# A transformer decoder layer on one core: all preparation two batches ahead and spread over four units, the first maxima cut on VectorE among zeros, the end worked by blocks, sums together behind the GELUs

## What is computed

```python
x = x + attn(_layernorm(x), wq, wk, wv, wo)          # rope, causal softmax
x = x + xattn(_layernorm(x), ctx_1024, ctx_1024, Wq, Wk, Wv, Wo, bq, bk, bv, bo)
x = x + ffn(_layernorm(x), W1, b1, W2, b2, scale)
# xattn, per batch and head (HEAD_DIM = 8, 256 queries, 1601 keys):
scores = jnp.einsum('bhqd,bhkd->bhqk', Q, K) * scale
attn = jax.nn.softmax(scores, axis=-1)
ctx = jnp.einsum('bhqk,bhkd->bhqd', attn, V)
# ffn: m1, m2 are outer products of tokens 1..16 of the batch
h = einsum(x, W1) + scale * einsum(x, m1) + b1
h = gelu(h)
out = einsum(h, W2) + scale * einsum(h, m2) + b2
```

## Time and profile before

| | |
|---|---|
| times of three runs | 397.19, 403.4, 404.17 us; median 403.4 |
| the profiled execution | 398.09 us, of it a span of 396.2 us from the first to the last instruction |
| TensorE's mean granted clock in it | 0.974 |
| busy share of the span | PE 91%, DVE 77%, ACT 75%, POOL 33% |
| clock at half | 55.98 to 69.6 us, and 342.7 to 349.5 us |

### The profile page before, as it was taken

One profiled execution on the slowest core, in us unless ns is written; L12 is line 12 of the kernel. 1 busy time (PEld: TensorE's weight loads), 2 busy tenths in 40 slices (PEclk: granted clock), 3 DMA queues, 4 the chain that ended last, 5 costly groups with the idle time before them and its releaser, 6 DMA issues.

```text
span 396.2 us, 11681 instructions
## 1 busy us (share of the span) xinstructions
PE 359.5 (91%) x4652; PEld 164.6 (42%) x4652; DVE 304.6 (77%) x694; ACT 298.3 (75%) x637; POOL 131.7 (33%) x204
## 2 busy tenths in 40 slices
PE   7777869989999989999998999999989999899976
PEld 3343433444543444444444434443434434253334
DVE  3566977779899988799998788999977999671022
ACT  1433246878889799889898798797998998859923
POOL 7711940389120206899200124373000037000010
PEclk9999985999999999999999999999999999789999
DMA  8366398013562212236400331114003310000000
GB/s 298 105 170 187 141 248 309 17 58 120 172 178 69 80 31 68 57 127 216 145 2 2 108 98 31 32 48 163 30 2 99 109 58 2 0 16 2 2 2 15
DMA packets 22300, 35.79 MB, mean 90 GB/s; under 512 B 1700, under 2 KB 19790, under 8 KB 22246
## 3 DMA queue, kind: packets, MB, share of 16 engines
q1 hardware_dynamic: 22246, 35.05, 28.4%
HBM read 19.25 MB, written 11.96 MB: 79 GB/s over the span
## 4 chain that ended last, share of the span: by engine, by line
PE 57%; DVE 16%; ACT 13%; issue 5%; POOL 4%; DMA 3%; SPq 0%; ACTq 0%; DVEq 0%; POOLq 0%
PE wsum L1053 20%; PE score L1067 13%; DVE part_max L722 11%; PE ring L1026 9%; PE ring L1087 9%; ACT probs L909 6%; DMA k_unit<-k_rows 2%; ACT q_unit L920 2%; POOL k_parts L570 2%; ACT prob_self L940 1%; PE ring L1112 1%; DMA x_all<-x 1%; PE ring L1137 1%; ACT hidden L997 1%; PE ring L1098 1%
## 5 line engine op out<-in xcount | busy, mean ns | idle before, releaser
L722 DVE TENSOR_REDUCE part_max<-ring 128x1 f32<-128x401 f32 x512 | 259.6, 567 | 35.9 <-PE ring L1087 34.4
L909 ACT ACTIVATE probs<-score 128x512 f32<-128x512 f32 (+1 forms) x416 | 222.6, 597 | 38.7 <-PE score L1067 34.9
L1087 PE MATMUL ring<-k_unit,q_unit 51*128 51x401 bf16 x512 | 141.6, 345 | 5.3 <-ACT v_aug L965 1.2
L1053 PE MATMUL wsum<-probs,v_unit 128*32 128x256 f32 (+1 forms) x1664 | 135.4, 394 | 2.1 <-ACT unit_ctx L914 2.1
L1067 PE MATMUL score<-q_unit,k_unit 51*128 51x256 bf16 (+1 forms) x832 | 124.0, 279 | 7.5 <-ACT probs L909 5.2
L1067 PEld LDWEIGHTS score<-q_unit,k_unit 51*128 51x128 bf16 (+1 forms) x832 | 47.4, 97 | 100.7 <-ACT probs L909 62.6
L1087 PEld LDWEIGHTS ring<-k_unit,q_unit 51*128 51x128 bf16 x512 | 47.7, 95 | 24.8 <-DVE part_max L722 13.2
L1053 PEld LDWEIGHTS wsum<-probs,v_unit 128*32 128x32 f32 (+1 forms) x1664 | 38.7, 109 | 41.5 <-issue 24.5
L570 POOL TENSOR_TENSOR max_parts<-neg_max,c_sb 128x8 bf16<-128x8 f32 x16 | 3.3, 209 | 130.9 <-DVE neg_max L726 130.8
L650 POOL TENSOR_SCALAR prob_norm<-prob_self,prob_rsum 128x128 f32<-128x128 f32 (+1 forms) x12 | 9.0, 763 | 42.9 <-DVE prob_rsum L802 42.9
L920 ACT ACTIVATE q_unit<-ring 3x512 bf16<-3x512 bf16 x32 | 18.5, 579 | 3.4 <-PE ring L1098 3.2
(11 more groups left out here) (115 smaller groups left out, 292.0 us busy)
## 6 DMA issues: line engine op xcount, KB each, us to landing
k_unit<-k_rows SPq DMA_DIRECT2D x32, 300.2 KB
v_unit<-v_aug SPq DMA_DIRECT2D x16, 234.0 KB, 6.7
ctx_sb<-ctx_t SPq DMA_DIRECT2D x4, 800.5 KB, 10.7
k_rows<-k_parts SPq DMA_DIRECT2D x3, 601.5 KB, 3.2
k_rows<-k_parts SPq DMA_DIRECT2D x3, 599.2 KB, 4.1
even<-ffn_rows SPq DMA_DIRECT2D x3, 512.0 KB, 3.9
q_unit<-q_rows SPq DMA_DIRECT2D x30, 48.0 KB
k_rows<-k_parts SPq DMA_DIRECT2D x3, 401.0 KB, 4.2
```

What stands on the lines that cost most here:

```text
L722: v_.tensor_reduce(part_max[:, par, q, head, hp, c:c + 1], ring[s][:, 0:CW], AX.X, ALU.max)\
L909: a_.activation(probs[0:rows, i % PB, :], score[i % EB][0:rows, :], ACT.Exp)\
L1053: last = mm(wsum[32 * j:32 * j + 32, 0:S], v_unit[0:rows, u, VQ * t + VW * j:VQ * t + VW * j + 32], probs[0:rows, i % PB, S * (j // 2):S * ...
L1087: mm(ring[s][:, 0:CW], q_unit[rows, u, hp, P * q:P * (q + 1)], k_unit[rows, u, L * hp + (CW - 1) * c:L * hp + (CW - 1) * c + CW], start=Tr ...
```

## The change

The preparation of batches 2 and 3, which stood one batch ahead for self-attention and two batches ahead for keys, values and rotary parts, now stands wholly two batches ahead, spread over the four quarters: offset 2 everywhere. Batch 1's self-attention goes into the start, among the 32 M of unit 0; its `x2T`, `q`, `split` and `store1` into unit 0 (`SIDE_FIRST`). So the units of batches 2 and 3 have no preparation left. New waits keep the single buffers safe. The load of the next batch's first keys and queries is an item of its own, `fetch`. The row maximum of self-attention is an item of its own, `rowmax`. `AHEAD` and `COUNT` are laid out anew. The first `neg_max` is cut into parts on VectorE instead of GpSimd, and 8 and 4 dummy multiplications of zeros stand ahead of and behind the first mT, instead of 2 ahead. Where the GELU's items stand, the three sums PV that would follow one by one stand together behind them (`sums_due`). At the end, `low0` is halved into two items, each hidden block `g0` to `g3` has a buffer and a GELU of its own, and the last product takes the blocks one by one, with two stores.

```diff
 SIDE = {
...
-    (1, 0): [("prep", "K2", 2)], (1, 1): [("prep", "wo", 1), ("post", "x3T", -1)], (1, 3): [("prep", "K3", 2)],
...
+    (1, 0): [("prep", "store0", 2)], (1, 1): [("prep", "e0", 2), ("prep", "e1", 2), ("prep", "rowmax", 2)],
+    (1, 2): [("post", "x3T", -1)], (1, 3): [("prep", "K2", 2)], (1, 4): [("prep", "soft", 2)],
+    (1, 6): [("prep", "pn", 2)], (1, 7): [("prep", "K3", 2)], (1, 8): [("prep", "v", 2)], (1, 9): [("prep", "fetch", 1)],
+    (1, 10): [("prep", "pT0", 2), ("prep", "pT1", 2)], (1, 11): [("post", "low", -1)],
...
+    (3, 0): [("ctx", 3), ("prep", "V3", 2)], (3, 3): [("post", "h0", -1), ("post", "h1", -1)], (3, 8): [("post", "out", -1)],
 }
+
+SIDE_FIRST = {0: [("prep", "x2T", 1)], 1: [("prep", "q", 1)], 4: [("prep", "split", 1)], 8: [("prep", "store1", 1)]}
...
-FIRST = [("keep", 20), ("ln1", 0), ("ln1", 1), ("xT", 0), ("qk", 0), ("qks", 0), ("K0", 0), ("K1", 0), ("keep", 5),
-         ("e0", 0), ("e1", 0), ("soft", 0), ("pn", 0), ("K2", 0), ("K3", 0), ("store0", 0), ("v", 0), ("xT", 1), ("keep", 6),
-         ("qk", 1), ("pT0", 0), ("pT1", 0), ("av", 0), ("store1", 0), ("wo", 0), ("U0", 0), ("U1", 0), ("U2", 0), ("U3", 0),
-         ("keep", 3), ("ln2", 0), ("x2T", 0), ("q", 0), ("split", 0), ("qks", 1), ("keep", 3), ("pick", 0),
-         ("U4", 0), ("U5", 0), ("U6", 0), ("load", 0), ("keep", 2)]
-BETWEEN = (("K0",), ("K1",), ("K2",), ("K3", "store0"), ("V0",), ("V1",), ("V2",), ("V3", "store1"))
-POST_LAST = ["OT", "Wo", "keep", "ln3", "x3T", "low0", "low1", "h0", "h1", "keep", "out"]
-KEEP_LAST = (10, 3)
-AHEAD = (14, 13, 7, 10)
-AHEAD_FIRST = 6
...
+FIRST = [("keep", 20), ("ln1", 0), ("ln1", 1), ("xT", 0), ("qk", 0), ("qks", 0), ("K0", 0), ("K1", 0), ("v", 0), ("xT", 1),
+         ("e0", 0), ("e1", 0), ("rowmax", 0), ("soft", 0), ("qk", 1), ("qks", 1), ("pn", 0), ("K2", 0), ("K3", 0),
+         ("store0", 0), ("keep", 4), ("pT0", 0), ("pT1", 0), ("av", 0), ("store1", 0), ("wo", 0),
+         ("e0", 1), ("e1", 1), ("U0", 0), ("U1", 0), ("ln2", 0), ("rowmax", 1), ("x2T", 0), ("q", 0), ("split", 0),
+         ("U2", 0), ("U3", 0), ("pick", 0), ("U4", 0), ("U5", 0), ("U6", 0), ("load", 0), ("soft", 1), ("v", 1)]
+BETWEEN = (("K0",), ("V0",), ("V1",), ("pn",), ("K1",), ("V2",), ("pT0",), ("pT1",), ("K2",), ("av",), ("V3",), ("wo",),
+           ("K3", "store0"), (), (), ())
+POST_LAST = ["OT", "Wo", "keep", "ln3", "x3T", "low0", "low1", "low2", "g0", "g1", "g2", "g3", "last"]
+KEEP_LAST = 10
+AHEAD = (14, 13, 11, 12)
+AHEAD_FIRST = 8
...
...
+def sums_due(v, t):
+    here, g = gelu_at(v), KT * v + t
+    since = [g - KT * w - gelu_at(w) for w in (v - 1, v) if 0 <= w and gelu_at(w) is not None and KT * w + gelu_at(w) <= g]
+    if here == t:
+        due = range(g - 3, g)
+    elif any(d in (1, 2) for d in since):
+        due = ()
+    else:
+        due = range(g - 3, g - 2)
+    return [("PV", *divmod(i, KT)) for i in due if i >= 0]
...
-    for i in range(MU // 4):
-        plan += [("M", 0, k) for k in range(4 * i, 4 * i + 4)] + [("prep", name, 1) for name in BETWEEN[i]]
+    for i in range(MU // 2):
+        plan += [("M", 0, 2 * i), ("M", 0, 2 * i + 1)] + [("prep", name, 1) for name in BETWEEN[i]]
     plan += [("ctx", 2)]
-    return plan + [("M", 1, k) for k in range(4)] + [("keep", 2), ("mT", 0)] + [("M", 1, k) for k in range(4, AHEAD_FIRST)]
+    return plan + [("M", 1, k) for k in range(4)] + [("keep", 8), ("mT", 0)] + [("M", 1, k) for k in range(4, AHEAD_FIRST)] + [("keep", 4)]
...
-                        if b:
-                            load_keys(b, 0)
-                            load_queries(b, 0)
-                        else:
+                        if b == 0:
                             load_rest(b)
+                    elif name == "fetch":
+                        load_keys(b, 0)
+                        load_queries(b, 0)
                     elif name == "load":
                         load_values(b, 0)
...
+                    if v == 0:
+                        dve.wait_ge(unit_max_done, 1)
+                        v_.tensor_copy(max_parts[:, :, 0], neg_max[:, 0, :]).then_inc(max_split, 1)
+                        dve.wait_ge(max_split, 1)
+                        v_.tensor_tensor(max_rest[:, :], neg_max[:, 0, :], max_parts[:, :, 0], ALU.subtract)\
+                            .then_inc(max_split, 1)
+                        dve.wait_ge(max_split, 2)
+                        v_.tensor_copy(max_parts[:, :, 1], max_rest[:, :]).then_inc(max_split, 1)
+                        dve.wait_ge(max_split, 3)
+                        v_.tensor_tensor(max_parts[:, :, 2], max_rest[:, :], max_parts[:, :, 1], ALU.subtract)\
+                            .then_inc(max_split, 1)
...
-                if kind == "M" and item[2] == MU - 1:
+                if kind == "M" and item[2] == MU - 1 and item[1]:
                     v = item[1]
                     pool.wait_ge(unit_max_done, v + 1)
-                    if v:
-                        s, n = RING["mT", v - 1]
-                        pool.wait_ge(drained[s], n + 1)
+                    s, n = RING["mT", v - 1]
+                    pool.wait_ge(drained[s], n + 1)
...
+                elif name[0] == "g":
+                    j = int(name[1])
+                    s, n = take(item)
+                    a_.activation(hidden[:, j, :], ring[s][:, 0:S], ACT.Gelu, bias=W("b1")[:, j:j + 1])\
+                        .then_inc(drained[s], 1)
...
+                elif name == "last":
+                    for j in range(FJ):
+                        for needed in ("low2", "g0") if j == 0 else (f"g{j}",):
+                            slot, m = RING["post", needed, pb]
+                            pe.wait_ge(drained[slot], m + 1)
+                        for q in range(QT):
+                            last = strips(score[1 + q][:, 0:D], hidden[:, j, P * q:P * (q + 1)],
+                                          w2_all[:, D * j:D * (j + 1)], start=j == 0, stop=j == FJ - 1)
+                            if j == FJ - 1:
+                                last.then_inc(last_sums, 1)
 
             pe.wait_ge(still_set, 1)
             keep(PLAN[0][1])
```

119 lines of the change are left out of this document (73 added, 46 removed).

## The result

The change is slower: 415.6 us (median of 4 runs, 413.0 to 419.2) against 402.9 of the kernel before on the same chip (397.2 to 404.2). The ratio is 1.0445, interval 1.0375 to 1.0514, which is some 18 us. The forecast of 398.5 (389 to 409) missed it. The profiled execution took 416.2 us, span 414.2, granted clock 0.934 (before: span 396.2, clock 0.974).

What follows compares the result with a forecast made beforehand. It took units to be bound by TensorE, VectorE or ScalarE by kind, with two half-clock stretches. Terms +4.3 -5.7 +0.5 -0.3 +6.3 -5.9 -0.2 -1.5 gave -2.5 from 398.1, 395.6; with half the scatter 398.5 us, range 389 to 409.

Steps and rivals of the forecast that it cites:

- the start: Up to the first score: batch 1's self-attention among the M makes it longer, +4.3 us (bounds +1.5 and +6).
- unit 0: Dummies ahead of it remove 13.6 us at half clock; 19.8 for 25.5 us, -5.7 (bounds 0 and -6.8).
- The wait at mT: Units 1 and 5: TensorE waits some 3 us each for GpSimd and at no other mT; +6.3 us (bounds 0, +9).
- rival 2: At mT in units 1 and 5 the clock falls at the new waits: 6.8 to 13.6 us, 405 to 412; chance 0.2.
- The last term: Start, neg_max to first score: cut of 0.9 covered by last M and eight dummies; 4.5 us in all, 0.7 more.
- The first term: Start, before unit 0's M: batch 1's added instructions lie where VectorE waits, so the keys' arrival does not change.
- the wait for the context: Unit 0: K0 of batch 2 waiting for its context, named as a sign of a wrong forecast, without a size.
- The gathered sums: GELU units, such as 7: sums behind the GELU fill a wait, at most one sum, 0.4 us.
- unit 6: V3 leaves (0.4), av, wo, x2T and q come (2.4 on TensorE): 21.8 for 20.2 us, +1.6.
- the end: After the last score unit: first GELU some 0.9 earlier, last product follows the GELUs; -1.5 us (bounds 0, -2.5).
- rival 1: At mT GpSimd is not late, or the wait is taken back: -8.8 to -11.6 us, 387 to 392; chance 0.25.
- rival 3: Start grows by its upper bound and the clock falls in unit 0 anyway: +4.9 us, 403; chance 0.1.

Runs made afterwards that it cites:

- e2: The change with 18 dummy multiplications of zeros ahead of mT's wait in units 1 and 5 alone; 410.7 us.
- e18: The change with only the gathered sums undone, the sums PV standing one by one; 411.9 us, ratio 1.0350 to the kernel before.
- e13: e1 plus early context load, K3's GpSimd split held behind the first cut, store0 moved, 2 dummies ahead of first mT, none behind, single sums; ratio 0.9986 to before.
- e1: The change with K3 (GpSimd's second key split) of quarter 1 moved from tile 7 to tile 11, behind the next unit's mT; 403.2 us.
- e4: The change with the two VectorE casts of the first maximum's cut written as adds of a zero column; 415.0 us.

## Why the prediction was wrong

The sum was -2.5 us and the profiles differ by +18.0. The miss of 20.5 lies in the start (4.8), unit 0 (4.6), units 1 to 3 and 4 to 7 (4.3 and 4.7) and units 8 to 11 (2.7), less 0.6 behind them. One thing runs through most of them: no term of the sum held any new half clock, and one counted on 13.6 us of it going away, while 34 us came.

- **The wait at mT** was forecast rightly in its place and cause, units 1 and 5, 3 us each; it measured 3.98 and 3.99. Against the forecast's "no other", one of 0.38 us stood at the end of unit 0. `pn` began 13.0 us into unit 1, not 11.5, and the cut was done at 23.7, not 22.3.
- **The clock behind it: the step that failed.** The sum took the two waits at their bare length and gave a fall behind them to rival 2, with a chance of 0.2. The clock fell at both, for 6.8 us each, and e2 shows that this cost some 5 us, 2.6 a stretch where the rival had 3.4. The rival compared the wait with the 2.1 busy us of 3.4 ahead of 342.7, and the wait gave 0.80 of 4.74. I had the numbers for that, a wait of 3 us for an engine that is otherwise full, and set against them that TensorE "idles too in GELU units without falling". Those idles are short and apart. By the forecast's own comparison this rival was the likeliest case; its 405 to 412 would still have missed, by the next terms.
- **The start**, +9.1 for +4.3. The M of unit 0 began 1.8 later (reductions from 37.41 for 35.57, forecast 0), took 4.1 longer (3.6), and from `neg_max` to the first score went 7.1 us instead of 4.0 (forecast 0.7 more). The last term failed most. The cut was priced at 0.9 and took 2.9, but the dummies ended 0.9 later still: priced at 0.27 us each, they took 0.45 at half clock, so mT came 3.8 us behind `neg_max` for 2.1, and the first score 3.1 behind mT for 2.4. The first term took for granted that the M wait for their keys. Before they did, until 35.19; in the change TensorE waited for VectorE's parts of the queries instead, which were done 2.7 us later than before (row below), and then worked without a gap up to `v` of batch 1, so that the M began at 37.03.

```profile
34.60 0.83 PE L1242 MATMUL ring<-q_parts,c_sb 128*128 128x256 bf16 x6 [1.37 <-DVE q_parts L835]
```

- **Unit 0**, -1.1 for -5.7. The dummies did not keep the clock: it fell at 56.0, ahead of them, and again at 69.7 in the wait for the context. That wait was named as what would make the forecast wrong, and was given no term. Ahead of 56.0 TensorE had been busy 2.7 of 3.5 us, far more than the 1.1 of before that the dummies were to fill; why the clock fell there no run shows. And the end of unit 0 stands behind the store, the key split and the cut, which the forecast did not have.
- **The gathered sums**, forecast 0.4 better a unit, cost 3.7 us (e18), by the falls. Unit 7 took 23.3 for the 21.6 forecast, unit 11 24.6 for 21.3. Without a fall (e13) units 8 to 11 took 6.0 us less than before, as forecast (5.9).
- **Right**: units 8 to 10, 16.6, 17.5 and 17.1 for 17.0, 17.4 and 17.4; unit 4, 19.7 for 20.3; unit 6, 22.2 with half clock in it and 22.1 without (e1), where its own terms (20.2 - 0.4 + 2.4) give 22.2 and not the 21.8 written; the end, -1.9 for -1.5, where the GELUs start at 408.47 and the last product 1.1 us later, not behind the last of them as in the earlier trace rows:

```profile
408.47 1.84 ACT L1054 ACTIVATE hidden<-ring,w_sb 128x256 f32<-128x256 f32 x4 [0.70 <-PE ring L1088]
409.57 1.96 PE L1088 MATMUL score<-w_all,hidden 128*32 128x128 f32 x64
```

Two of the rivals' times leave out the half of the scatter that the others hold: with it rival 1 reaches down to 389, not 387, and rival 3 comes to 406, not 403. Nothing above hangs on it.

Open are why the clock falls at 56.0, why the store of batch 1's keys is late, what moving the split behind it would give, and whether gathering costs anything on the kernel before.

## What to carry over

When a wait is forecast on a nearly full TensorE, count the busy time in the few us around it and look for stretches in the trace of before that were as empty; if they were followed by half clock, the fall belongs into the likeliest sum, not into a rival. That catches the falls at such waits, not every one. A light engine (GpSimd, 32% busy) is late where long items stand ahead of a short one that others wait for: put the long ones behind it, and after each move read the whole queue of that engine anew, not only the item moved. And work that fills an engine's waits was worth most spread out here; collected in one place, it made one long wait of several short ones.

## What I had not expected of the hardware

A VectorE instruction of 128x8 elements takes 0.17 to 0.18 us beside an idle GpSimd and up to 1.57 beside GpSimd's key split, where it ended only when GpSimd's own instruction had ended (59.09 and 59.05, 60.89 and 60.86); a cast and an addition fare alike (the change, e4). VectorE's reductions from PSUM beside the same split kept their 0.5 us (six in 3.08 us from 61.01 on). Dummy multiplications cost double at half clock: 0.45 us each ahead of the first mT, 3.6 us for eight, where 18 of them took some 3.8 us at full clock in e2.
